# Moving the next sequence's output projection ahead of the previous tail's last norm, a reordered begin and a fifth ring slot

## Chip, cores and metric

One core of a Trainium2 chip runs the kernel. The metric is the device time of one execution in microseconds (us): the median over the runs of the kernel before is 3390.8 us, the lowest is 3381.3 and the highest 3396.3.

## The reference

The input x is four sequences of 512 tokens with 512 channels, and there is a second input ctx with 256 channels. Six blocks follow each other, each with a residual and a layer norm:

```python
x = _layernorm(x + _L0_attn_ref(x, ...))            # gated state-space scan + output projection, then an FFN (1408)
x = _layernorm(x + _L0_xattn_ref(ctx_1024, x, ...)) # scan over ctx, 512 channels, gated by silu(x)
x = _layernorm(x + _L0_ffn_ref(x, ...))             # 8 experts, top 2, and a shared expert
x = _layernorm(x + _L1_attn_ref(x, ...))            # attention inside segments of 4 tokens
x = _layernorm(x + _L1_xattn_ref(x, ctx_1024, ...)) # x mixed with softmax(query @ key.T) of ctx
x = _layernorm(x + _L1_ffn_ref(x, ...))             # top-8 router, scales x and adds a bias row
```

The scans are `h = exp(dt * A) * h + dt * B * u; y = sum_n h * C` over time, with 16 states for each channel.

## The kernel before

The kernel works through four sequences b = 0 to 3. A sequence has three parts. The **front** norms x (tasks p_sq and p_nrm), projects it (p_mm, 16 chunks of 128 channels), convolves (p_ev) and makes dt, B and C. A short front for ctx (c_load, c_mm, c_ev, c_th, c_bc) does the same for the second scan. The **scans** are three units of 512 channels (unit q = 3b is the ctx scan, 3b + 1 and 3b + 2 are the two halves of the x scan), each with 16 steps, one for each state: on the vector engine (DVE) a step is the multiply by B (L1303), the scan itself (L1386) and the multiply by C (L1394); TensorE (PE) spreads the rows of B (L675) and C (L781) over the partitions into PSUM; the scalar engine (ACT) makes the exponentials (L1007); GpSimd (POOL) adds up over states (L1664). A unit opens with dt_mm, dt_exp, dt_b and dt_c and, for the x units, ends with fin (L1398), which gates the result into `yg`.

The **tail** of a sequence is one long dependent chain: the output projection mix (L804, eight half-chunks of eight matmuls), x1 (L1413, adds x), t_sq and t_rs (mean of squares with a matmul by ones, L811, and the norm, L1419), the FFN (L830 and L837 up, L665 down), two layer norms, the gate, routing (L907), 15 expert blocks (transposes L847, gate and up L854 and L858, down L873), the shared expert (L665), the segment attention (L951, L962), xmix (L968), norm 4, the router of the last block (bias_a, L975), bias_b and bias_c (L987), bias_d (adds L1600, statistics L1604), bias_y (L1613) and the output (L592). In tail b the first matmul of mix waits for the statistics of bias_d of tail b - 1, because both use PSUM banks 0 to 4, and x1 and t_rs wait for the previous output, which is stored from T2.

All four engines run instructions strictly in an order that `plan()` and `schedule()` write at build time: `plan()` lists tasks with a rank (lower goes first), a duration and predecessors, and `schedule()` simulates a list scheduler. The semaphore waits in the code keep it right whatever the durations are. While tail b runs, the scans of sequence b + 1 and its front run too, on the same engines. Weights stream from HBM on the sync engine's (SP) queue into a ring of NSLOT slots of 512 KB; a load waits until the slot's last user is done. On the same queue stand the outputs and, once, the relay: 57 copies from DRAM to DRAM (`egu`, `xrows`) that lay out the expert weights, placed between the sixteen loads of fold. Fold (L789, L791) folds attention weights once, after the front of sequence 0. At the start SP loads `pk` (constants) and `eb`; ACT loads X, then a few small pieces, waits for the DVE set-up to finish (`set`), and only then issues the loads of hx (V) and ctx (L1028, L1034). c_mm of sequence 0 uses one PSUM bank for its four chunks and waits for each convolution; dt_mm does the same with bank 5.

Buffers that matter: V holds the residual sum x1, then hx of the next front, ctx and the attention matrix of xmix; T2 holds the normed input and then `nat`, the running value of the tail; T1 holds FFN temporaries, p_sq's squares and the scaled value of bias_b.

Of the kernel before, what the change touches and what calls it, by code (L numbers as in the profile page):

```python
# [16 lines left out]
P = 128  # L17
# [21 lines left out]
NSLOT, SLOT = 4, 1024  # L39
# [16 lines left out]
for _n, _c in _PACK:  # L56
# [9 lines left out]
       "h_done": 2, "delta": 3, "hx_in": 16, "ctx_in": 16, "tctx_in": 16, "x_in": 16, "out_done": 16 * TT,  # L66
# [15 lines left out]
def plan():  # L82
# [16 lines left out]
    for q in range(UNITS):  # L99
# [3 lines left out]
        for k in range(4):  # L103
            after = [(("dt_mm", q, k - 1), "act")] if k else [last, ready, (("sa", first - 2, 0), "act") if q else None]
            chain(15, ("dt_mm", q, k), [("pe", 0.9), ("act", 1.45)], *after)
# [65 lines left out]
    for b in range(SEQS):  # L171
        at = (("bias_d", b - 1, 0), "dve") if b else (("folded", 0, 0), "dve")
        for m in range(2 * KC):
            at = chain(30, ("mix", b, m), [("pe", 3.6)], at, (("fin", 3 * b + 2, 0), "dve"))
            if m % 2:
                chain(30, ("x1", b, m // 2), [("dve", 0.7)], at, (("bias_y", b - 1, 0), "dve") if b else None)
        if b:
            put(30, ("out", b - 1, 0), "pe", 0, (("mix", b, 2 * KC - 1), "pe"))
# [3 lines left out]
        at = chain(30, ("t_rs", b, 0), [("act", 2.7), ("dve", 2.9)], (("t_sq", b, 0), "pe"))  # L182

        def hidden(kind, chunks, at, us):

            for c in chunks:
                wait = []
                if c - 2 >= chunks[0]:
                    wait.append(((kind + "_ev", b, c - 2), "dve"))
                put(30, (kind + "_mm", b, c), "pe", 3.6, at, *wait)  # L190
# [3 lines left out]
                      (("c_bc", 1, 0), "dve") if kind == "ffn" and b == c == 0 else None)  # L194
# [52 lines left out]
        for k in range(FA):  # L247
# [14 lines left out]
        chain(60, ("att_qk", b, 0), [("pe", 5), ("act", 1.4)], (("t_load", b, 0), "act", 4),  # L262
              (("p_gz", b + 1, 2 * UC - 1), "dve") if b + 1 < SEQS else None)
        row = (("att_qk", b, 0), "act")
# [28 lines left out]
def lender(task):  # L293
# [5 lines left out]
    if t in ("p_bc", "p_bb") and n == 0:  # L299
        return t, b, 1  # L300
    if t in ("dt_mm", "c_mm") and n == 0:
# [5 lines left out]
    return task if t in ("c_bc", "fold", "att_qk", "bg", "bd") else None  # L307


def schedule():  # L310
# [44 lines left out]
    [f"slot{i}" for i in range(NSLOT)] + ["pk_in", "memz", "pm_in", "aneg", "set"] +  # L355
    ["x_in", "hx_in", "ctx_in", "tctx_in", "out_done"] +
# [14 lines left out]
def build(nc, pack, w_in, w_x, w_bc, w_dt, x_in_w, x_proj_w, x_dt_w, w_out, w_fgu, w_fdn, w_egu, w_edn,  # L371
# [3 lines left out]
    with ExitStack() as ctx:  # L375
# [61 lines left out]
        att, nat, ynat = V, T2, T2  # L437
# [1325 lines left out]
```

## Time and profile before

| what | value |
|---|---|
| median of 3 runs | 3390.8 us |
| profiled execution, time | 3388.9 us |
| profiled execution, span | 3387.1 us |
| PE busy | 2446.5 us (72%) |
| DVE busy | 2505.5 us (74%) |
| ACT busy | 1237.5 us (37%) |
| POOL busy | 1049.0 us (31%) |
| mean granted TensorE clock | 0.825 |
| mix of sequence 0 starts (L804) | 640.3 us |
| unit 5 ends (L1398) | 1319.5 us |
| unit 8 ends | 1999.0 us |
| unit 11 ends | 2717.6 us |
| scan instructions L1386 | 192, mean 4511 ns |

The spans are those of one profiled execution. A window row gives the stretch, its length, and then for each engine the busy time and in brackets the number of instructions, then the granted clock (1.00 is full, 0.50 is half), the mean busy share of the 16 DMA engines and what they moved. A chain row is one piece of the chain of work that ended last. In a timeline row the bracket at the end gives how long the engine stood idle before it and what released it.

### The profile page before, as it was taken

How to read it: one execution, taken by the hardware profiler on the slowest of the kernel's cores; microseconds unless marked ns; L12 is line 12 of the kernel's file. 1: busy time of each engine (PE TensorE's matmuls, PEld its weight loads, DVE VectorE, ACT ScalarE, POOL GpSimd, SP SyncE). 2: the span in 40 equal slices, each digit the busy share in tenths (PEclk: the TensorE clock that was granted, in tenths of full speed). 3: DMA queues.
4: the chain of work that ended last, by engine and by line, in shares of the span. 5: the costliest groups of instructions: out<-in, count | busy, mean ns of one | idle time of the engine just before them, and what ended most of it. 6: DMA issues, size and time to landing. Idle time of an engine off the chain costs nothing. (4 is left out here: it accounts for less than half of the span.)

```text
span 3387.1 us, 20370 instructions
## 1 busy us (share of the span) xinstructions
PE 2446.5 (72%) x6316; PEld 1167.2 (34%) x6316; DVE 2505.5 (74%) x1928; ACT 1237.5 (37%) x1970; POOL 1049.0 (31%) x291
## 2 busy tenths in 40 slices
PE   4775121589788864699787865699788867979875
PEld 1232000234344432334433432344434433444432
DVE  2986989899699988996988979966989922121023
ACT  3433232443534534344425454324434322021122
POOL 0233544434245353332344433412353410000000
PEclk8775555699889976799889986799799977979986
DMA  2163000111226630122126630122136611215730
GB/s 85 33 194 109 0 6 0 31 59 55 69 74 207 212 106 6 50 64 69 50 97 202 201 104 0 51 71 72 40 121 208 205 55 50 69 46 192 252 112 13
DMA packets 151196, 307.87 MB, mean 91 GB/s; under 512 B 29808, under 2 KB 47216, under 8 KB 150000
## 3 DMA queue, kind: packets, MB, share of 16 engines
q1 hardware_dynamic: 130864, 261.41, 24.8%
q10 hardware_dynamic: 15104, 28.38, 2.4%
q0 software_dynamic: 5120, 16.78, 1.5%
q8 instruction: 51, 0.84, 0.1%
q14 instruction: 57, 0.47, 0.0%
HBM read 278.21 MB, written 43.78 MB: 95 GB/s over the span
## 5 line engine op out<-in xcount | busy, mean ns | idle before, releaser
L1664 POOL TENSOR_TENSOR ya<-ya,hb 128x2048 f32<-128x2048 f32 x188 | 859.8, 4574 | 1375.7 <-DVE hb L1386 1295.7
L1386 DVE TENSOR_TENSOR_SCAN hb<-da,hb 128x2048 f32<-128x2048 f32 x192 | 866.1, 4511 | 1.3
L1007 ACT ACTIVATE da<-dl,pk 128x511 f32<-128x511 f32 x768 | 489.3, 710 | 562.2 <-DVE hb L1386 545.5
L1303 DVE TENSOR_TENSOR hb<-du,ps 128x2048 f32<-128x2048 f32 x192 | 435.7, 2269 | 28.8 <-PE ps L675 17.2
L1394 DVE TENSOR_TENSOR hb<-hb,ps 128x2048 f32<-128x2048 f32 x192 | 437.4, 2278 | 0.6
L675 PE MATMUL ps<-bct,sel 64*128 64x512 f32 x192 | 112.2, 584 | 332.1 <-DVE hb L1303 327.1
L704 PE MATMUL ps<-V,ring 128*128 128x512 f32 x512 | 246.0, 634 | 23.7 <-DVE ucv L1284 13.0
L665 PE MATMUL ps<-ring,hid 128*128 128x512 f32 x544 | 242.5, 600 | 3.2 <-ACT X L1172 1.6
L854 PE MATMUL ps<-ring,hid 128*128 128x352 f32 x480 | 199.6, 499 | 48.7 <-DMA ring<-egu 40.5
L858 PE MATMUL ps<-ring,hid 128*128 128x352 f32 x480 | 193.0, 485 | 12.3 <-ACT X L1172 11.9
L675 PEld LDWEIGHTS ps<-bct,sel 64*128 64x128 f32 x192 | 40.8, 213 | 459.4 <-DVE hb L1303 369.7
L781 PE MATMUL ps<-bct,sel 64*128 64x512 f32 x192 | 105.2, 548 | 127.3 <-DVE hb L1394 127.1
L873 PE MATMUL ps<-ring,X 128*128 128x512 f32 x360 | 177.1, 625 | 11.9 <-DMA ring<-in_w_edn 10.1
L830 PE MATMUL ps<-T,ring 128*128 128x512 f32 x352 | 167.1, 619 | 16.8 <-DVE T L1419 16.4
L837 PE MATMUL ps<-T,ring 128*128 128x512 f32 x352 | 159.1, 594 | 0.0
L704 PEld LDWEIGHTS ps<-V,ring 128*128 128x128 f32 x512 | 101.8, 204 | 157.7 <-issue 147.4
L665 PEld LDWEIGHTS ps<-ring,hid 128*128 128x128 f32 x544 | 101.9, 191 | 134.8 <-issue 129.4
L998 ACT ACT_TABLE_LOAD x44 | 56.5, 1283 | 237.8 <-DVE mv L1254 179.8
L1436 DVE SCALAR_TENSOR_TENSOR T<-T,ps 128x352 f32<-128x352 f32 x60 | 30.5, 509 | 141.7 <-ACT T L1160 141.7
L804 PE MATMUL ps<-yg,ring 128*128 128x512 f32 x256 | 121.8, 636 | 11.1 <-DVE sm L1604 10.1
L1649 POOL TENSOR_TENSOR dl<-dl,hb 128x2048 f32<-128x2048 f32 x12 | 57.3, 4779 | 231.5 <-ACT hb L1118 231.5
L1149 ACT ACTIVATE T<-ps 128x512 f32<-128x512 f32 x68 | 40.3, 596 | 240.0 <-PE ps L830 239.8
(242 smaller groups left out, 3439.6 us busy)
## 6 DMA issues: line engine op xcount, KB each, us to landing
ring<-egu SPq DMA_DIRECT2D x240, 352.0 KB, 3.4
ring<-in_w_edn SPq DMA_DIRECT2D x72, 512.0 KB, 4.9
ring<-in_w_fgu SPq DMA_DIRECT2D x44, 512.0 KB, 3.6
ring<-in_w_in SPq DMA_DIRECT2D x32, 512.0 KB, 3.6
hid<-xrows SPq DMA_DIRECT2D x60, 256.0 KB, 3.5
yrows<-X ACTq DMA_DIRECT2D x60, 256.0 KB, 4.2
ring<-in_w_egu SPq DMA_DIRECT2D x24, 512.0 KB, 3.3
ring<-in_w_edn SPq DMA_DIRECT2D x60, 192.0 KB, 4.4
```

The costliest lines, as they stand in the source:

```text
L665: i = pe.matmul(ps[:, e, :], hid[:, k - lo, e * P:(e + 1) * P], cur["down"][:, base:base + HID], start=(k == lo), stop=(k == hi - 1 and do ...
L704: i = pe.matmul(ps[:, 4 + 2 * (n % 2), :], cur["w"][:, o:o + P], hx[:, k, :], start=(k == 0), stop=(k == KC - 1))
L830: i = pe.matmul(ps[:, b0, :], w[:, k * P:(k + 1) * P], src[:, k, :], start=(k == 0), stop=(k == KC - 1))
L837: i = pe.matmul(ps[:, 2 * (n % 2) + 1, :], cur["gu"][:, o:o + P], src[:, k, :], start=(k == 0), stop=(k == KC - 1))
L854: pe.matmul(ps[:, 2 * (j % 2), 0:FE], xt(j)[:, k * P:(k + 1) * P], w[:, 0:FE], start=(k == 0), stop=(k == KC - 1))
L858: pe.matmul(ps[:, 2 * (j % 2) + 1, 0:FE], xt(j)[:, k * P:(k + 1) * P], w[:, FE:2 * FE], start=(k == 0), stop=(k == KC - 1)).then_inc(s["bg ...
L873: x = pe.matmul(ps[:, 2 * (j % 2) + 1, :], ht_(j)[0:rows, f:f + P], w[0:rows, o:o + HID], start=(i == 0), stop=(i == len(FB) - 1))
L1007: i = act.activation(dav(n % 2)[:, k, 1:], dl[:, k, 1:], ACT.Exp, scale=Aneg[:, (4 * (u % 3 - 1) if u % 3 else UC) + k, m:m + 1])
L1303: dve.tensor_tensor(hbv(m % NHB), du[:, :, :], wide(ps[:, 5, :], 4), ALU.mult).then_inc(s["dbu"], 1)
L1386: dve.tensor_tensor_scan(hb[:, h, :], da[:, b % 2, :], hb[:, h, :], 0.0, ALU.mult, ALU.add)\
L1394: dve.tensor_tensor(hbv(h), hbv(h), wide(ps[:, 7, :], 4), ALU.mult).then_inc(s["hc"], 1)
L1664: pool.tensor_tensor(sums, ya[:, :, :], hbv(m % NHB), ALU.add).then_inc(s["acc"], 1)
```

## The change

The ring gets a fifth slot. At the begin, ACT issues the loads of ctx and hx first, X follows later, and `eb` and the whole relay move behind the load of dt_mm of unit 2. In sequence 0, c_mm and dt_mm of unit 0 use four PSUM banks. The output projection of sequence b may start as soon as xmix of tail b - 1 is done (and fin, and the next ctx front): it uses banks 4 and 6 in turn, its x1 adds in place to a copy of x that a new load x_load brings into V, the squares go to `hid`, their sum to bank 4. The output is stored from T1, so waits for the stored output move from x1 and t_rs to the next front's p_sq and the FFN's first two chunks; the FFN's first matmul takes over the wait for bias_d. att_qk becomes two tasks, with the same instructions. The diff, cut to its core ("..." marks what is left out of a line):

```diff
-NSLOT, SLOT = 4, 1024
+NSLOT, SLOT = 5, 1024
@@ plan(): dt_mm, c_mm
-            after = [(("dt_mm", q, k - 1), "act")] if k else [last, ready, ...]
+            after = [(("dt_mm", q, k - 1), "act" if q else "pe")] if k else [last, ready, ...]
-            put(60, ("c_mm", b, n), "pe", 1.8, (("c_ev", b, n - 1), "dve") if n else (("c_load", b, 0), "act", 4),
+            put(60, ("c_mm", b, n), "pe", 1.8, (("c_ev", b, n - 1), "dve") if n and b else (("c_load", b, 0), "act", 4), ...
@@ plan(): output projection
-        at = (("bias_d", b - 1, 0), "dve") if b else (("folded", 0, 0), "dve")
+        at = (("xmix", b - 1, TT - 1), "pe") if b else (("folded", 0, 0), "dve")
+        put(30, ("x_load", b, 0), "act", 0.1, (("xmix", b - 1, TT - 1), "pe") if b else (("p_mm", 0, 2 * UC - 1), "pe"))
-            at = chain(30, ("mix", b, m), [("pe", 3.6)], at, (("fin", 3 * b + 2, 0), "dve"))
+            at = chain(30, ("mix", b, m), [("pe", 3.6)], at, (("fin", 3 * b + 2, 0), "dve"),
+                       (("x1", b, m // 2 - 2), "dve") if m >= 4 else None,
+                       (("c_bc", b + 1, 0), "dve") if b + 1 < SEQS else None)
-                chain(30, ("x1", b, m // 2), [("dve", 0.7)], at, (("bias_y", b - 1, 0), "dve") if b else None)
-        if b:
-            put(30, ("out", b - 1, 0), "pe", 0, (("mix", b, 2 * KC - 1), "pe"))
+                chain(30, ("x1", b, m // 2), [("dve", 0.7)], at, (("x_load", b, 0), "act", 4.5))
-        at = chain(30, ("t_rs", b, 0), [("act", 2.7), ("dve", 2.9)], (("t_sq", b, 0), "pe"))
+        at = chain(30, ("t_rs", b, 0), [("act", 2.7), ("dve", 2.9)], (("t_sq", b, 0), "pe"),
+                   (("bias_b", b - 1, 0), "act") if b else None)
+        if b:
+            put(30, ("out", b - 1, 0), "pe", 0, (("bias_y", b - 1, 0), "dve"))
@@ hidden(): the first two FFN chunks of b
+                    wait.append((("bias_d", b - 1, 0), "dve"))
@@ build(): storage, loads
-        att, nat, ynat = V, T2, T2
+        att, nat, ynat = V, T2, T1
+                    if b == 2:
+                        n += [("relay", e, 0) for e in range(EXP)]
-                    if i % 2:
-                        n.append(("relay", i // 2, 0))
-                sp.dma_start(eb[:, :], ebias).then_inc(s["pk_in"], 16)
+                            sp.dma_start(eb[:, :], ebias).then_inc(s["eb_in"], 16)
@@ tensor engine
-                        else:
+                        elif b:
                             pe.wait_ge(*of("h_conv", b, n))
-                            i = pe.matmul(ps[:, 6, :], cur["c"][:, o:o + P], cx(b)[:, k, :],
+                            i = pe.matmul(ps[:, 6 if b else n, :], cur["c"][:, o:o + P], cx(b)[:, k, :],
-                        pe.matmul(ps[:, 5, :], cur["d"][0:rows, n * P:(n + 1) * P], low[0:rows, :],
+                        pe.matmul(ps[:, 5 if q else n, :], cur["d"][0:rows, n * P:(n + 1) * P], low[0:rows, :],
@@ tensor engine, mix
-                            if b:
-                                pe.wait_ge(*of("bn", b - 1, 1))
+                            if b + 1 < SEQS:
+                                pe.wait_ge(*of("h_bc", b + 1, 2))
+                        elif half == 0 and m >= 2:
+                            pe.wait_ge(*of("x1", b, m - 1))
-                            i = pe.matmul(ps[:, m, :], cur["mix"][:, k * P:(k + 1) * P], yg[:, k, :],
+                            i = pe.matmul(ps[:, 4 + 2 * (m % 2), :], cur["mix"][:, k * P:(k + 1) * P], yg[:, k, :],
@@ t_sq
-                            i = pe.matmul(ps[:, 0, :], ones, T1[:, k, :], start=(k == 0), stop=(k == KC - 1))
+                            i = pe.matmul(ps[:, 4, :], ones, hid[:, k, :], start=(k == 0), stop=(k == KC - 1))
@@ ffn_mm, n == 0
+                                if b:
+                                    pe.wait_ge(*of("bn", b - 1, 1))
@@ scalar engine
-                act.dma_start(X[:, :, :], xT[0]).then_inc(s["x_in"], 16)
+                act.dma_start(cx(0), ctxT[0]).then_inc(s["ctx_in"], 16)
+                act.dma_start(hx[:, :, :], xT[0]).then_inc(s["hx_in"], 16)
@@ p_sq, n == 0
-                            if b:
-                                act.wait_ge(*of("stat", b - 1, 1))
+                            if b >= 2:
+                                act.wait_ge(*of("out_done", b - 2, 16 * TT))
+                    elif t == "x_load":
+                        if b:
+                            act.wait_ge(*of("down", b - 1, 16))
+                        else:
+                            act.wait_ge(*of("h_mm", b, 20))
+                        act.dma_start(V[:, :, :], xT[b]).then_inc(s["xv_in"], 16)
@@ ffn_ev, first two chunks
+                        elif b:
+                            act.wait_ge(*of("out_done", b - 1, 16 * TT))
@@ vector engine, x1 and t_rs
-                        dve.tensor_tensor(V[:, n, :], ps[:, n, :], X[:, n, :], ALU.add).then_inc(s["x1"], 1)
+                        dve.tensor_tensor(V[:, n, :], ps[:, 4 + 2 * (n % 2), :], V[:, n, :], ALU.add).then_inc(s["x1"], 1)
-                            dve.wait_ge(*of("out_done", b - 1, 16 * TT))
+                            dve.wait_ge(*of("xs", b - 1, TT))
@@ gpsimd, t_sq
+                        pool.wait_ge(*of("x_in", b, 16))
```

## Rows read from the trace of the kernel before

**Rows 1.** Windows: busy us of each engine, granted clock, DMA share, GB/s.

```profile
200.00:285.00 85.00, 67.66 (x176) 37.91 (x174) 65.54 (x40) 19.78 (x31) 32.24 (x7) 0.55 0.78 223
285.00:640.00 355.00, 79.33 (x98) 25.55 (x98) 317.35 (x111) 119.70 (x172) 163.37 (x38) 0.51 0.02 6
1330.00:1404.00 74.00, 44.62 (x111) 22.83 (x110) 69.55 (x68) 25.21 (x44) 22.73 (x6) 0.64 0.04 15
1404.00:1600.00 196.00, 184.61 (x421) 76.90 (x421) 159.58 (x112) 83.75 (x117) 63.26 (x14) 0.97 0.22 72
2120.00:2300.00 180.00, 150.12 (x331) 62.72 (x331) 135.13 (x126) 57.23 (x83) 49.87 (x10) 0.88 0.19 61
2715.00:2838.00 123.00, 70.52 (x202) 41.44 (x201) 40.35 (x90) 31.20 (x63) 9.90 (x9) 0.69 0.12 39
3081.00:3247.00 166.00, 136.97 (x447) 73.88 (x445) 16.31 (x31) 33.10 (x62) 0.00 (x0) 0.98 0.76 240
```

**Rows 2.** Chain of waits, sequences 2 to 3: start, us, what.

```profile
2783.26 16.83 PE ps L968 x32
...
2813.38 7.10 PE ps L975 x32
2827.56 7.21 PE ps L987 x8
...
2838.14 30.40 PE ps L804 x64
2868.54 3.45 PE ps L811 x8
2875.57 6.42 PE ps L830 x8
```

**Rows 3.** Timeline of the begin: start, us, engine, line, operation [idle before].

```profile
18.07 0.45 ACTq L1034 DMA_DIRECT2D hid<-in_ctxT  x1
27.68 0.78 ACT L1066 ACTIVATE yb<-ps,pk 128x512 f32<-128x512 f32 x1 [13.91 <-PE ps L743]
28.50 2.31 DVE L1284 SCALAR_TENSOR_TENSOR yb<-ps,pk,yb 128x511 f32<-128x511 f32 x3 [10.84 <-ACT yb L1066]
34.58 0.78 ACT L1066 ACTIVATE yb<-ps,pk 128x512 f32<-128x512 f32 x1 [3.11 <-PE ps L743]
...
51.58 5.25 PE L751 MATMUL ps<-yb,ring 128*64 128x512 f32 x8 [3.27 <-issue]
...
70.98 5.86 PE L704 MATMUL ps<-V,ring 128*128 128x512 f32 x8
...
96.00 4.42 DVE L1386 TENSOR_TENSOR_SCAN hb<-da,hb 128x2048 f32<-128x2048 f32 x1
```

**Rows 4.** DVE's waits, window 96 to 285: total us, times, longest.

```profile
DVE hb L1303 <- PE ps L675: 17.2, 4, 9.1
```

**Rows 5.** Page, DMA issues: count, KB each, us to landing.

```profile
ring<-in_w_in SPq DMA_DIRECT2D x32, 512.0 KB, 3.6
ring<-in_w_qo SPq DMA_DIRECT2D x16, 512.0 KB, 5.9
```

**Rows 6.** Timeline of the change from sequence 0's tail to 1's.

```profile
1344.64 3.17 PE L968 MATMUL ps<-V,X 128*128 128x512 f32 x7
...
1399.23 12.48 PE L804 MATMUL ps<-yg,ring 128*128 128x512 f32 x24 [3.38 <-DVE sm L1604]
...
1447.85 2.90 PE L830 MATMUL ps<-T,ring 128*128 128x512 f32 x3 [4.27 <-DVE T L1419]
```

**Rows 7.** The same change, sequence 1's tail to 2's.

```profile
2092.50 3.17 PE L968 MATMUL ps<-V,X 128*128 128x512 f32 x7
...
2149.53 2.90 PE L804 MATMUL ps<-yg,ring 128*128 128x512 f32 x3 [3.38 <-DVE sm L1604]
```

**Rows 8.** PE's waits, window 3081 to 3247.

```profile
PE ps L854 <- DMA ring<-egu: 23.9, 15, 2.7
```

**Rows 9.** A window of 2 us within one block of the last tail.

```profile
3126.00:3128.00 2.00, 0.84 (x3) 0.64 (x4) 0.00 (x0) 0.00 (x0) 0.00 (x0) 1.00 1.01 340
```

More of the change, by code:

```diff
@@ L103, in plan @@
         for k in range(4):
-            after = [(("dt_mm", q, k - 1), "act")] if k else [last, ready, (("sa", first - 2, 0), "act") if q else None]
+            after = [(("dt_mm", q, k - 1), "act" if q else "pe")] if k else [last, ready, (("sa", first - 2, 0), "act") if q else None]
             chain(15, ("dt_mm", q, k), [("pe", 0.9), ("act", 1.45)], *after)
@@ L300, in lender @@
         return t, b, 1
+    if t == "att_qk" and n == 0:
+        return t, b, 1
     if t in ("dt_mm", "c_mm") and n == 0:
@@ L353 @@
 SIGNALS = (
-    [f"slot{i}" for i in range(NSLOT)] + ["pk_in", "memz", "pm_in", "aneg", "set"] +
-    ["x_in", "hx_in", "ctx_in", "tctx_in", "out_done"] +
+    [f"slot{i}" for i in range(NSLOT)] + ["pk_in", "eb_in", "memz", "pm_in", "aneg", "set"] +
+    ["x_in", "xv_in", "hx_in", "ctx_in", "tctx_in", "out_done"] +
     ["h_stat", "h_mm", "h_tr", "h_tstat", "h_bstat", "h_dtm", "b_row", "c_row",
@@ L920, in _ @@
                     elif t == "att_qk":
-                        w = slot()
-                        pe.wait_ge(*of("tctx_in", b, 16))
-                        if b + 1 < SEQS:
-                            pe.wait_ge(*of("h_gz", b + 1, UC))
-                        if b + 2 < SEQS:
-                            pe.wait_ge(*of("h_bc", b + 2, 2))
-                        for g in range(2):
-                            if g:
-                                pe.wait_ge(*of("qk_sb", b, 1))
-                            for k in range(CC):
-                                o = (g * CC + k) * P
-                                i = pe.matmul(ps[:, 6, :], w[:, o:o + P], tcx[:, k, :],
-                                              start=(k == 0), stop=(k == CC - 1))
-                            i.then_inc(s["qk"], 1)
+                        if n == 0:
+                            cur["qk"] = slot()
+                            pe.wait_ge(*of("tctx_in", b, 16))
+                            if b + 1 < SEQS:
+                                pe.wait_ge(*of("h_gz", b + 1, UC))
+                            if b + 2 < SEQS:
+                                pe.wait_ge(*of("h_bc", b + 2, 2))
+                        else:
+                            pe.wait_ge(*of("qk_sb", b, 1))
+                        for k in range(CC):
+                            o = (n * CC + k) * P
+                            i = pe.matmul(ps[:, 6, :], cur["qk"][:, o:o + P], tcx[:, k, :],
+                                          start=(k == 0), stop=(k == CC - 1))
+                        i.then_inc(s["qk"], 1)
                     elif t == "att_row":
@@ L1064, in _ @@
                                 act.wait_ge(*of("g2", b - 2, TT))
-                            dst, bank, w, bias = yb(b)[:, n, :], 6, "conv_wB", "conv_bB"
+                            dst, bank, w, bias = yb(b)[:, n, :], 6 if b else n, "conv_wB", "conv_bB"
                         act.activation(dst, ps[:, bank, :], ACT.Identity, bias=c(bias, n),
@@ L1101, in _ @@
                         act.wait_ge(s["h_dtm"], 4 * q + n + 1)
-                        act.activation(dl[:, n, :], ps[:, 5, :], ACT.Relu, bias=bias)
-                        act.activation(hbv(1)[:, n, :], ps[:, 5, :], ACT.Abs, bias=bias).then_inc(s["dt_abs"], 1)
+                        bank = 5 if q else n
+                        act.activation(dl[:, n, :], ps[:, bank, :], ACT.Relu, bias=bias)
+                        act.activation(hbv(1)[:, n, :], ps[:, bank, :], ACT.Abs, bias=bias).then_inc(s["dt_abs"], 1)
                     elif t == "skip":
@@ L1199, in _ @@
                     elif t == "att_qk":
-                        for g, (dst, bias) in enumerate(((qT, "bq"), (kT, "bk"))):
-                            act.wait_ge(*of("qk", b, g + 1))
-                            act.activation(dst, ps[:, 6, :], ACT.Identity, bias=c(bias)).then_inc(s["qk_sb"], 1)
+                        dst, bias = ((qT, "bq"), (kT, "bk"))[n]
+                        act.wait_ge(*of("qk", b, n + 1))
+                        act.activation(dst, ps[:, 6, :], ACT.Identity, bias=c(bias)).then_inc(s["qk_sb"], 1)
                     elif t == "att_row":
```

58 lines of the change are left out of this document (32 added, 26 removed).

## The prediction

> **What bounds the kernel now.** I read the windows first [rows 1]. They show two regimes. Up to 2715 us DVE is the busiest engine, but not evenly: it works 94% of the stretch 1330 to 1404 (69.55 of 74 us) and only 81% of 1404 to 1600 (159.58 of 196) and 75% of 2120 to 2300 (135.13 of 180), where PE is at 94% and 83%. After 2715 there are no scans left, DVE idles, and what remains is the dependent chain of tail 2's end and of tail 3. So the kernel is bound by DVE where scans are ready, by the tail's own latency elsewhere, and the stretches in which DVE idles come right after an output projection: the scans of the ctx unit run out before the next front, which waits for the projection and its norm, has delivered.
>
> Second, the chain of waits [rows 2]. Between sequences 2 and 3 it is PE alone, one piece behind the other: xmix ends at 2783.26 + 16.83 = 2800.1, mix starts at 2838.14 and the first FFN matmul at 2875.57. The reader should see two serial pieces, 38.0 us of last norm, router and bias, and 37.4 us of mix (30.40), squares (3.45) and norm, which have no data in common. In the window 2715 to 2838 PE is busy for 57% (70.52 of 123). The same two pieces stand after the earlier tails: sequence 0 to 1, 1347.8 to 1399.2 to 1447.9, or 51.4 and 48.6 us [rows 6]; sequence 1 to 2, 2095.7 to 2149.5, or 53.8 us [rows 7]. They are longer there because scans share the engines.
>
> **The begin.** ACT issues the ctx load at 18.07, after the DVE set-up, though nothing needs to hold it; the first ACT evacuation comes at 27.68 [rows 3]. With ctx on its way from the first microsecond ACT can start it when it is free, about 17.7: 10 us earlier. Then the four chunks follow each other every 6.9 us (34.58 less 27.68), since the next matmuls wait for the convolution. With a bank for each only DVE is serial: 2.31 us of convolution and some 0.7 for the product (an estimate by the size of the 512-column operations), 3.05 per chunk, so 17.7 + 0.8 + 4 x 3.05 = 30.7 instead of 51.58 for the next matmul, 20.9 us. dt_mm of unit 0 in four banks saves a little more, but the first scan at 96.00 stands behind convolutions of the x front, which begins at 70.98 and moves with the same 21 us. I take 21. Bounds: 10 if only the load helps, 27 if dt_mm adds all it can. Up to the first mix nothing but the chain of DVE follows, so the gain passes on. The x load, moved ahead of the small loads, is twice the size of ctx; if it delays the constants, that is the lower bound.
>
> **The relay.** In 200 to 285 DVE is busy for only 65.54 of 85 us, the DMA share is 0.78 and they move 223 GB/s [rows 1]. The fold loads land in 5.9 us, where equal ones take 3.6 [rows 5]; PE waits for them, the row matmul L675 stands behind in PE's order, and DVE waits 17.2 us for it [rows 4]. Without the 57 copies between them, the folds wait little. What remains is at most one fold ahead of a row matmul, so I take 11 of the 17.2; bounds 0 and 17. The copies themselves, some 15 MB or 70 us at 223 GB/s, go to a stretch of 355 us with a DMA share of 0.02 [rows 1]. On SP they stand ahead of the load of unit 3 and of mix's weights, which are wanted only at about 600. They cost nothing there; if that cover were gone, the 70 us would stand before the first mix. `eb` is read first in the last bias step of tail 0: nothing.
>
> **The projection, sequence 3.** From 2800.1, PE has to do ln_t (3.7, an estimate by its 16 transposes), bias_a 7.10, bias_b about 1, bias_c 7.21, mix 30.40 and squares 3.45 [rows 2]: 52.9 us. After bias_c DVE still adds and takes the statistics, about 3.3, before the FFN may touch banks 0 to 3; a piece of mix, 3.8 us, may stand before a piece of the chain once or so. The FFN then starts at about 2800.1 + 52.9 + 3.3 + 2 = 2858.3 instead of 2875.57: 17 us. Bounds: 8, if the squares and the norm (7.0 from 2868.54 to 2875.57) come last, and 24, if no piece delays another and the fuller PE shortens its own matmuls.
> That last point is a clock matter: the window 2715 to 2838 shows a granted clock of 0.69, a mean of the two levels 1.2 and 2.4 GHz, with PE idle for 43%; 1404 to 1600, with PE at 94%, shows 0.97 [rows 1]. The Trainium skill, "TensorE: Matmul & The Clock Gate", section "What's actually happening", says that the default state is throttled and activity releases it. By that rule the interleaved router and bias matmuls would run at the upper level and sequence 3 would give some 4 us more; the sum doesn't use it.
>
> **Sequences 1 and 2.** Here the norm chain (51.4 and 53.8) and the projection chain (48.6) also lie side by side now. PE has room while the norm runs (44.62 of 74 busy [rows 1]). The FFN's start moves by 48.6 less some 9 us of interleaving: 39. But DVE can't give all of it: what it idles from 1330 to 1600 is 4.5 + 36.4 = 40.9 us, and a full DVE still idles 3 to 6%. 229.1 us of work at 94% take 243.7, a gain of 26; I take 27. For sequence 2 the idle time is 44.9 in 2120 to 2300 alone, 135.13 us at 94% take 143.8, a gain of 36; the chain gives at most 39, and x1 and the normed input now fall into DVE's full stretch, so I take 30. Bounds: 0 and 39 for each. Sequence 0 has no tail in front: nothing.
> New waits. PE waits for x1 of two chunks before, and behind it stand the row matmuls of the scans. x1 comes 7.6 us of matmuls earlier, and a scan on DVE takes 4.4, so this costs little. ACT's p_sq waits for the stored output of the tail before, with the exponentials behind it; the output follows bias_y, which is over by then if the order is roughly kept. SP's output wait moves ahead of some FFN loads; the fifth slot is ahead of it. POOL's wait for X is for a load issued in bias_b, long landed. x_load adds 4 MB in stretches with a DMA share of 0.04 to 0.12. All these at nothing, at most 3 us each.
>
> **The fifth slot.** In tail 3's expert blocks PE waits 23.9 us for gate and up weights, 15 times [rows 8]. The windows show the DMA engines at 0.76 and 240 GB/s in the mean [rows 1] but at 1.01 and 340 GB/s while PE waits [rows 9]: they are full in bursts and idle between, because a load can't start before a slot is free. A slot more fills the troughs, but can't make the bursts faster. I take 14, bounds 0 and 24. In the other tails DVE hides most; I take nothing.
> The Trainium skill, "DMA: Bandwidth & Descriptors", section "Specifications", gives about 358 GB/s as the HBM limit of a core; the 340 measured here agree. By that rule the mean could still rise from 240 by up to 49%, and the slot would take all 24 us; the sum keeps 14.
>
> **Sum.** 21 + 11 + 27 + 30 + 17 + 14 = 120 us off the profiled 3388.9, or 3268.9. The median before is 1.9 above the profiled run: **3271 us**, 3.5% faster. By the bounds of each, with not all at one end, this case reaches from 3235 to 3310.
>
> **Rivals.**
> - *DVE gives it back.* The projection moves, but the scans of sequences 1 and 2 lose in the norm's stretch what they win later, as DVE is 94% busy there. Against it stand the 25% idle of 2120 to 2300. It costs 57: 3328, from 3310 to 3350.
> - *The order doesn't do it.* The new list keeps the projection's pieces behind the norm's, all of rank 30. Then 74 us go: 3345. If the front's later place also eats the begin's gain, it ends at about 3375.
> - *More than the sum.* The earlier front also starts the x units earlier and closes idle time outside the windows that I counted, and each part comes near its upper bound: 3215.
> - *Slower.* p_sq's wait for the stored output stands on ACT before the exponentials, the output stands behind bias_y on a full DVE, and SP waits for it before it loads FFN weights. Each scan step that DVE misses costs 9 us (2.3 + 4.4 + 2.3). It decides from 5 missed steps at each of the three boundaries on, 45 x 3 = 135 against 120; at 6 it gives 3271 + 162 = 3433. Its ground is that ACT's order is fixed; against it, bias_y needs only bias_d's statistics and a short norm, and mix and its norm took 48.6 us from there to the FFN [rows 6].
>
> **How the numbers follow.** Chances: forecast 0.57, given back 0.18, order 0.10 (half of it near no change), more 0.08, slower 0.07. About 0.5%, 17 us, is what a measurement of this kernel can tell from no change. So faster 0.88, same 0.05, slower 0.07. The range 3225 to 3345 holds the forecast, nearly all of the first rival and part of the third.
>
> **What would show it.** Begin: the first scan near 75 us instead of 96, the first mix near 608 instead of 640. Relay: no 17 us wait for L675, and a DMA share above 0.15 in 285 to 450. Projection: matmuls L804 right after xmix, between those of L975 and L987, and the FFN of sequence 3 58 us after xmix instead of 75. DVE above 88% after the second and third mix. The slot: PE's wait for gate and up weights near 10 us in the last tail. I am wrong if the periods from mix to mix, 750 us now, shrink by less than 15, if p_sq or x1 shows a wait of tens of us, or if the tail of sequence 3 keeps its length.

## The result, and the profile after

| | before | after |
|---|---|---|
| median of all runs on the same chip | 3388.5 us | 3244.2 us (3241.5 to 3250.0) |
| ratio, with its 95% interval | | 0.9576 (0.9550 to 0.9603) |
| profiled execution | 3388.9 us, span 3387.1 | 3242.2 us, span 3240.4 |

The change takes 144 us off, 4.2%; 120 were forecast, and the time lies in the range. Where it came from shows in the milestones of each sequence, read from the timelines (us from the start of the span; "xmix" is the end of the tail's last matmul group, "mix" and "FFN" are the first matmuls of the output projection and of the FFN that follow):

| | first scan | mix 0 | FFN 0 | xmix 0 | FFN 1 | xmix 1 | FFN 2 | xmix 2 | FFN 3 | end |
|---|---|---|---|---|---|---|---|---|---|---|
| before | 96.0 | 640.3 | 689.9 | 1347.8 | 1447.8 | 2095.7 | 2198.2 | 2800.1 | 2875.6 | 3387.1 |
| after | 62.3 | 602.9 | 652.5 | 1300.0 | 1362.4 | 2015.9 | 2078.4 | 2701.1 | 2750.9 | 3240.4 |

Differences of neighbours give the sum: 37.4 up to the first mix and 10.4 in tail 0. The three stretches from xmix to FFN shrink by 37.6, 40.0 and 25.7. Tails 1 and 2 then give back 5.6 and 20.8 (647.9 to 653.5, 601.9 to 622.7), and tail 3 is 22.0 shorter. Together 146.7, the difference of the two spans.

The windows of after, over the stretches that answer to [rows 1] (start:end, length, busy us and number of instructions of PE, weight loads, DVE, ACT, POOL, granted clock, DMA share, GB/s):

```profile
200.00:285.00 85.00, 59.28 (x163) 33.45 (x162) 62.22 (x39) 30.64 (x41) 32.43 (x8) 0.63 0.57 177
285.00:450.00 165.00, 33.17 (x40) 11.01 (x40) 151.03 (x52) 54.94 (x80) 77.23 (x18) 0.50 0.22 59
1362.00:1560.00 198.00, 190.08 (x455) 81.42 (x455) 174.70 (x123) 87.89 (x126) 63.51 (x15) 0.98 0.25 82
2078.00:2260.00 182.00, 173.25 (x391) 71.93 (x391) 148.09 (x106) 76.51 (x106) 50.08 (x12) 0.98 0.26 82
2684.00:2751.00 67.00, 57.86 (x165) 27.77 (x165) 25.83 (x62) 18.52 (x32) 4.50 (x1) 0.91 0.19 63
2953.00:3092.00 139.00, 130.24 (x443) 72.48 (x442) 16.32 (x31) 32.56 (x61) 0.00 (x0) 1.00 0.90 287
```

The relay's copies now run from 255.8 to 317.7, behind the fold's loads. PE is nearly full after each boundary (96 and 95%), and DVE, at 81 and 75% before, is at 88% (174.70 of 198) and still only 81% (148.09 of 182) in the same places. The next to last row is the end of tail 2 with the projection of sequence 3 in it: PE busy for 86% at a clock of 0.91. (Between xmix and the end of the projection alone, 2701 to 2738, the granted clock is 1.00; from xmix to mix before, 2800 to 2838, it was 0.53.) In the last row the DMA engines move 287 GB/s through tail 3's blocks, 240 before.

The chain of waits at that boundary (start, us, what; mix is now L815, xmix L980, the norm's transposes L905, the router L987, the last bias steps L993 and L1000, the FFN L842), against [rows 2]:

```profile
2684.11 16.99 PE ps L980 x32
2701.09 10.30 PE ps L815 x24
2711.39 1.75 PE ps L905 x16
2713.14 3.44 PE ps L815 x8
2716.58 3.52 PE ps L987 x32
2720.10 6.92 PE ps L815 x16
2727.02 0.44 PE ps L993 x4
2727.46 3.44 PE ps L815 x8
2730.89 3.64 PE ps L1000 x8
...
2735.28 2.48 DVE sm L1629 x4
...
2743.67 1.46 DVE T L1638 x3
...
2745.63 5.21 DMA ring<-in_w_fgu
...
2750.88 5.73 PE ps L842 x8
```

The projection's pieces (L815) lie between those of the norm and the router, as the list of the change says. The group L987 takes 3.52 and L1000 3.64, where the same groups took 7.10 and 7.21 when they stood alone. And a link is there that the forecast did not have: before the FFN PE waits for its weights, not for the norm (8.25 us of idle time, ended by the load).

### The profile page after: what moved, and what is told of

Read it like the earlier page. It is cut to its first block, busy times and chain, and to the rows that moved or that the text cites. A ratio compares the mean times of both kernels' runs of the same rounds, so it can differ in the third digit from the quotient of the medians.

```text
span 3240.4 us, 20396 instructions
## 1 busy us (share of the span) xinstructions
PE 2410.5 (74%) x6316; PEld 1156.1 (36%) x6316; DVE 2482.0 (77%) x1928; ACT 1236.3 (38%) x1970; POOL 1044.1 (32%) x291
## 4 chain that ended last, share of the span: by engine, by line
PE 35%; DVE 31%; issue 18%; ACT 9%; DMA 4%; POOL 3%; ACTq 0%; SPq 0%; DVEq 0%; POOLq 0%
DVE hb L1413 12%; PE ps L842 6%; PE ps L849 6%; DVE hb L1421 4%; DVE hb L1330 4%; PE ps L713 3%; PE ps L674 3%; DMA ring<-in_w_edn 2%; PE ps L885 2%; PE ps L980 2%; POOL ya L1690 2%; PE ps L776 2%; DVE sm L1274 1%; PE ps L815 1%; DVE hb L1396 1%
## 5 line engine op out<-in xcount | busy, mean ns | idle before, releaser
L1330 DVE TENSOR_TENSOR hb<-du,ps 128x2048 f32<-128x2048 f32 x192 | 435.9, 2270 | 33.1 <-POOL ya L1690 25.2
L713 PE MATMUL ps<-V,ring 128*128 128x512 f32 x512 | 242.7, 627 | 25.7 <-DVE yg L1371 11.0
L842 PE MATMUL ps<-T,ring 128*128 128x512 f32 x352 | 166.9, 619 | 23.9 <-DVE T L1444 15.6
L713 PEld LDWEIGHTS ps<-V,ring 128*128 128x128 f32 x512 | 100.4, 201 | 155.6 <-issue 134.8
L674 PEld LDWEIGHTS ps<-ring,hid 128*128 128x128 f32 x544 | 102.4, 191 | 138.5 <-issue 132.6
L870 PEld LDWEIGHTS ps<-ring,hid 128*128 128x128 f32 x480 | 94.8, 203 | 83.4 <-ACT X L1199 33.8
L815 PE MATMUL ps<-yg,ring 128*128 128x512 f32 x256 | 116.1, 607 | 0.9 <-DVE yg L1425 0.9
```

Of the source, the lines that this page charges most:

```text
L674: i = pe.matmul(ps[:, e, :], hid[:, k - lo, e * P:(e + 1) * P], cur["down"][:, base:base + HID], start=(k == lo), stop=(k == hi - 1 and do ...
L713: i = pe.matmul(ps[:, 4 + 2 * (n % 2), :], cur["w"][:, o:o + P], hx[:, k, :], start=(k == 0), stop=(k == KC - 1))
L842: i = pe.matmul(ps[:, b0, :], w[:, k * P:(k + 1) * P], src[:, k, :], start=(k == 0), stop=(k == KC - 1))
L870: pe.matmul(ps[:, 2 * (j % 2) + 1, 0:FE], xt(j)[:, k * P:(k + 1) * P], w[:, FE:2 * FE], start=(k == 0), stop=(k == KC - 1)).then_inc(s["bg ...
L1330: dve.tensor_tensor(hbv(m % NHB), du[:, :, :], wide(ps[:, 5, :], 4), ALU.mult).then_inc(s["dbu"], 1)
```

## The experiments

All are the kernel after with one part undone, unless another base is named. "After" is the profiled execution above. Differences of spans and milestones compare one execution with one other, and some of them are scatter: in seven kernels whose begin is that of after, or differs from it only by the number of slots, the first mix lies anywhere from 602.1 to 610.3 us and the first scan from 62.0 to 65.7. The ratios are each to runs of the kernel before on the same chip; that of after is 0.9576 (0.9550 to 0.9603).

### The projection back behind the norm, in all boundaries, in two, in one

```diff
-        at = (("xmix", b - 1, TT - 1), "pe") if b else (("folded", 0, 0), "dve")
+        at = (("bias_d", b - 1, 0), "dve") if b == 3 else (("xmix", b - 1, TT - 1), "pe") if b else (("folded", 0, 0), "dve")
```

This is the kernel for sequence 3 alone; the others have `b` (all) and `0 < b < 3` in place of `b == 3`.

> The changed kernel, only its plan is altered: the projection of sequences 1, 2 and 3 is listed behind bias_d of the tail in front, as before; storage, waits, ring and begin stay changed. My theory (the gain lies in the order): in the changed kernel the stretch from xmix's end to the next FFN shrank by 37.6, 40.0 and 25.7 us and tails 1 and 2 gave 5.6 and 20.8 back, so this kernel loses 77: about 3321 us, with the first projection unmoved at about 603 us. Rival 1 (the separate storage does it and the order hardly matters): 3244 to 3255. Rival 2 (what was given back came from something else, the order is worth the full 103): 3347.

Measured: 3331.6 us, ratio to before 0.981 (0.978 to 0.984), span 90.4 above after. Of these, 7.4 stand before the first mix (610.3), where this edit changes nothing; behind it 83.0 are left.

> The changed kernel with the projections of sequences 1 and 2 alone listed late. Theory (the two give 77.6 us at their place, and DVE takes 26 of them back in tails 1 and 2, where it then has more scans left): 3244 + 51 = 3295. Rival 1 (they pass on in full): 3322. Rival 2 (where scans run DVE is the bound and nothing passes on): 3244 to 3255.

Measured: 3303.0 us, 0.972 (0.969 to 0.975), span 64.8 above. xmix to FFN is 34.3 and 41.7 longer (FFN at 1396.7 and 2161.0), 76 in all; at xmix 2 64.7 are left, at 2765.8 instead of 2701.1. The tails take back only 11, not the 26 expected: tail 2 takes 604.8, 18 less than in after, but tail 1 takes 660.1, nearly 7 more.

> The changed kernel with the projection of sequence 3 alone listed late. No scans are left here, so what it gave at its place passes on: 25.7 us, about 3270. Of these I take 18 for matmuls in idle time and 7 for the clock: then the last router and bias matmuls of tail 2, L987 and L1000, are back at about 7 us each from 3.7. Rival (the clock had another cause): those stay at 3.7 and the kernel is at 3262.

Measured: 3265.5 us, 0.962 (0.959 to 0.964), span 24.0 above. xmix 2 ends at 2701.3, as in after, and the FFN starts 73.2 us behind it instead of 49.8. Its chain of waits, same columns as above:

```profile
2684.31 17.00 PE ps L980 x32
...
2714.62 7.10 PE ps L987 x32
...
2728.80 7.19 PE ps L1000 x8
2735.99 30.46 PE ps L815 x64
...
2774.52 5.37 PE ps L842 x8
```

The two long durations are back, and the granted clock from xmix to mix (2701 to 2736) is 0.54, as it was before. The parts give 64.8 + 24.0 = 88.8, all three together 90.4, or 83.0 from the first mix on. So the order by itself is worth 83 to 90 us of the 147 in these profiles. The ratios, 0.981 against 0.958, say 79.

### Do idle matmuls give the clock's share without the projection?

On the kernel before, matmuls whose result nobody reads, ahead of the norm's last group, of bias_a and of bias_b, in the tails of sequences 2 and 3 (the last of the three places is shown; the others have 12 and 4 matmuls):

```diff
+                        if b >= 2:
+                            for _ in range(10):
+                                pe.matmul(ps[:, 6, :], ones, fill512, start=True, stop=True)
```

> The kernel before, with matmuls that compute nothing of use put into PE's idle time in the last norm and router of tails 2 and 3 (12, 4 and 10 of 128x512, into a bank that nobody reads), the result unchanged. Theory of the clock (idle PE is why L975 and L987 took 7.1 and 7.2 us, and interleaved work is why they take 3.7 in the changed kernel): in tail 2 they go to 3.7 each, in tail 3 to 3.7 from 5.4 and 7.2, in all 12 us: 3388 less 12 = 3376. Rival (the clock has another cause, or the added matmuls delay the chain as much as they give): 3388 or more.

Measured: 3388.3 us, 0.998 (0.997 to 1.000). Its chain of waits (here the fillers are L893, L978 and L988, router and bias L982 and L997, mix L805):

```profile
2799.40 10.30 PE ps L893 x24
...
2811.45 3.44 PE ps L978 x8
2814.88 3.52 PE ps L982 x32
2818.40 8.64 PE ps L988 x20
...
2828.25 3.71 PE ps L997 x8
...
2835.33 29.78 PE ps L805 x64
```

The durations fall as expected, 7.10 to 3.52 and 7.21 to 3.71, and the granted clock of the stretch is 0.96 instead of 0.53. But from xmix's end to mix it takes 35.9 us instead of 38.0, and to the FFN 72.7 instead of 75.5: of some 7 us that the groups save only 2.8 arrive. PE runs its instructions in order, so 10.30 + 3.44 + 8.64 us of fillers stand in the chain themselves, where only part of that was idle before. The profiled span is 11.7 us shorter all the same, but this execution lies 11 us under the median of ten, and 5.0 of it come from the last tail's blocks (146.8 us from the first to the last matmul of the down projections, instead of 151.8), where no filler runs. The ratio says 0.2%, by its interval 0.0 to 0.3%. So the 12 us expected did not come, and the rival, that the added matmuls cost about what they give, was nearer: I had counted them as filling waits alone. In the change the fillers are work that has to be done anyway; that the same effect is worth its full size there is argued from this, no run separates it.

### The give-back: is tail 2 longer because DVE is full?

In the C multiply of all three units of sequence 3 only a quarter of the channels is multiplied (this leaves out a part of the scan's output), so each of these 48 multiplies takes 0.68 us instead of 2.28, and DVE has less to do beside tail 2:

```diff
-                        dve.tensor_tensor(hbv(h), hbv(h), wide(ps[:, 7, :], 4), ALU.mult).then_inc(s["hc"], 1)
+                        m4 = 1 if b >= 9 * NST else 4
+                        dve.tensor_tensor(hbv(h)[:, 0:m4], hbv(h)[:, 0:m4], wide(ps[:, 7, :], m4), ALU.mult).then_inc(s["hc"], 1)
```

> The changed kernel in which the 48 scan steps of sequence 3 multiply only a quarter of the channels by C (a part of its scan output is not computed): 48 x 1.7 = 80 us less for DVE, nearly all inside tail 2. Theory (tail 2 became 20.8 us longer, 622.7 from FFN start to xmix end, since 48 us more of DVE work fall into it): tail 2 shrinks by 30 us or more, to under 595, kernel about 3244 less 35 = 3209. Rival (PE or the loads made tail 2 longer, DVE is not its bound): tail 2 stays within 8 us of 622.7.

Measured: 3213.0 us, 0.947 (0.944 to 0.949). FFN 2 starts at 2074.9 and xmix 2 ends at 2676.5: 601.6 us, against 622.7 in after and 601.9 in before. The window 2078 to 2626, first of this kernel, then of after:

```profile
2078.00:2626.00 548.00, 464.08 (x1259) 222.29 (x1257) 448.14 (x341) 233.29 (x376) 214.81 (x60) 0.92 0.39 124
```

```profile
2078.00:2626.00 548.00, 472.31 (x1246) 224.75 (x1246) 484.86 (x326) 222.48 (x351) 211.89 (x60) 0.92 0.39 124
```

With 36.7 us less on DVE in this window, tail 2 gives back nothing. The 21.1 us are short of the 30 expected, and far outside the rival's 8. More of the scans fall into tail 2 of after: 39 scan steps start in it, 34 in before, and DVE works 509.6 us in it, against 461.8 in before and 463.9 in this kernel. The length goes with DVE's work; PE is at 85 and 86% in the two windows. For tail 1 this is not shown: it gave back 5.6, but with the projections late (x_late_b12 above) DVE had 8 us less to do in it and it took 6.7 us longer still. That part stays open.

### The fifth slot

On after, `NSLOT` 5 to 4:

> The changed kernel with four ring slots, for the loads and for the plan. Theory: the fifth slot is worth what tail 3's expert blocks lost, 27 us from 166 to 139, and some of the 10 us by which tail 0 is shorter: 3244 + 27 to 37 = 3271 to 3281, and PE waits about 24 us for gate and up weights in the blocks of tail 3. Rival (DMA was at its limit and the shorter blocks come from the clock or chance): 3244 to 3255.

Measured: 3265.6 us, 0.963 (0.960 to 0.966), span 21.7 above, and the last tail's blocks (first to last down matmul, as above) take 147.6 us instead of 125.2. On before, the slot alone, with the plan still made for four (`NSLOT` 5, and `len(lent) >= 4`, `lent[-4]` in the function that makes it):

> The kernel before with a fifth ring slot in storage and loads, its plan unchanged (it still plans with four). Theory: the slot alone takes 22 to 27 us off tail 3's expert blocks and little elsewhere: 3388 less 22 = 3366, PE's wait for gate and up weights in the blocks of tail 3 falls from 23.9 to about 2. Rival (it needs the new order): 3380 to 3388.

Measured: 3364.6 us, 0.992 (0.989 to 0.995), span 27.7 below before, and the last tail's blocks take 127.5 us instead of 151.8. PE's waits over those blocks (line waited at, for what: total us, times, longest), in this order: after, after with four slots, before with five:

```profile
PE ps L885 <- DMA ring<-in_w_edn: 6.2, 10, 1.4
PE ps L866 <- DMA ring<-egu: 1.6, 3, 0.8
```

```profile
PE ps L866 <- DMA ring<-egu: 23.1, 16, 2.5
PE ps L885 <- DMA ring<-in_w_edn: 3.8, 4, 1.6
```

```profile
PE ps L873 <- DMA ring<-in_w_edn: 4.9, 8, 1.3
PE ps L854 <- DMA ring<-egu: 3.1, 6, 1.0
```

From either side the slot is worth 22 to 24 us in the blocks, all of [rows 8], and 22 to 28 in the whole span. With four slots xmix 0 also ends 7.6 us later than in after, most of the 10.4 that tail 0 gained; but before with five slots has the same tail 0 as before (657.7 us), so the slot does this only together with the rest of the change. xmix 2 is only 0.7 later (2701.8): tails 1 and 2 have made it up by then, through what is not shown.

### The three parts of the begin

Relay copies back between the fold loads:

```diff
-                    if b == 2:
-                        n += [("relay", e, 0) for e in range(EXP)]
...
+                    if i % 2:
+                        n.append(("relay", i // 2, 0))
```

> The changed kernel with the relay's copies between the fold loads again. Theory: DVE waits some 17 us for L684 again in the fold, the first projection comes 11 us later than 602.9, and the kernel is at 3244 + 11 = 3255, less what DVE slack absorbs. Rival (with five slots the folds are fed anyway): first projection within 3 us of 602.9, 3244.

Measured: 3250.5 us, 0.958 (0.956 to 0.961); first mix at 609.3, 6.4 later than after. That is within the scatter named above. Counted from the first scan on, which takes part of the scatter out, this kernel takes 547.3 us to the first mix, the ten others with the copies moved 539.4 to 544.9. The loads of fold land in 6.1 us here, in 3.4 in after, as in 5.9 before [rows 5]. DVE's wait for the row matmul, by relay back, then in after (window 60 to 285):

```profile
DVE hb L1330 <- PE ps L684: 8.3, 3, 4.2
```

```profile
DVE hb L1330 <- PE ps L684: 5.5, 3, 2.9
```

It was 17.2 in before [rows 4]. The larger part of that wait is gone even with the copies in the old place. Either edit alone does that. Before with five slots, copies and begin as they were, has the first row for 96 to 285; after with four slots, copies moved, has the second for 60 to 285:

```profile
DVE hb L1303 <- PE ps L675: 9.6, 4, 4.3
DVE hb L1330 <- PE ps L684: 4.5, 3, 2.9
```

The ctx and x loads back behind the set-up, X first:

```diff
-                act.dma_start(cx(0), ctxT[0]).then_inc(s["ctx_in"], 16)
-                act.dma_start(hx[:, :, :], xT[0]).then_inc(s["hx_in"], 16)
+                act.dma_start(X[:, :, :], xT[0]).then_inc(s["x_in"], 16)
```

> The changed kernel with the loads of ctx and hx issued behind the DVE set-up again and X first, banks as changed. Theory: the first evacuation of ctx comes at about 28 us instead of 19.6, everything up to the first projection moves by these 8 to 10 us: first projection at about 612, kernel 3253. Rival (the load order is hidden by the set-up): first projection 603, 3244.

Measured: 3250.4 us, 0.958 (0.955 to 0.960); first mix at 611.2, 8.3 later. The first evacuation comes 8.0 us later than in after (27.61 for 19.61). The first evacuation and the first scan of this kernel (start, us, engine, line, operation, idle before):

```profile
27.61 0.78 ACT L1083 ACTIVATE yb<-ps,pk 128x512 f32<-128x512 f32 x1 [13.78 <-PE ps L752]
...
70.73 4.42 DVE L1414 TENSOR_TENSOR_SCAN hb<-da,hb 128x2048 f32<-128x2048 f32 x1
```

One PSUM bank again for the four chunks of the ctx front and for unit 0's dt matmuls:

```diff
-                            i = pe.matmul(ps[:, 6 if b else n, :], cur["c"][:, o:o + P], cx(b)[:, k, :],
+                            i = pe.matmul(ps[:, 6, :], cur["c"][:, o:o + P], cx(b)[:, k, :],
...
-                        pe.matmul(ps[:, 5 if q else n, :], cur["d"][0:rows, n * P:(n + 1) * P], low[0:rows, :],
+                        pe.matmul(ps[:, 5, :], cur["d"][0:rows, n * P:(n + 1) * P], low[0:rows, :],
```

with the waits and predecessors that belong to one bank.

> The changed kernel with one PSUM bank for c_mm of sequence 0 and dt_mm of unit 0 again, loads as changed. Theory: the four chunks take 6.9 us each again instead of 3: the next matmul is 12 us later and the first scan, with dt_mm in one bank, 16 to 20 us later than 62.3; first projection at about 617, kernel 3258. Rival (DVE is the bound up to there, so an earlier first scan is only an earlier first scan): first projection within 4 us of 602.9.

Measured: 3264.6 us, 0.962 (0.959 to 0.964), span 22.7 above; first mix at 627.4, 24.5 later, where 617 was expected. The timeline of the begin, first with one bank, then in after:

```profile
19.65 0.78 ACT L1082 ACTIVATE yb<-ps,pk 128x512 f32<-128x512 f32 x1 [4.30 <-DVE T L1351]
26.33 0.78 ACT L1082 ACTIVATE yb<-ps,pk 128x512 f32<-128x512 f32 x1 [2.89 <-PE ps L752]
...
43.10 5.21 PE L760 MATMUL ps<-yb,ring 128*64 128x512 f32 x8 [3.27 <-issue]
...
62.46 5.84 PE L713 MATMUL ps<-V,ring 128*128 128x512 f32 x8
...
62.56 0.69 ACT L1119 ACTIVATE dl<-ps,pk 128x512 f32<-128x512 f32 x1 [2.16 <-PE ps L776]
...
87.47 4.43 DVE L1413 TENSOR_TENSOR_SCAN hb<-da,hb 128x2048 f32<-128x2048 f32 x1
```

```profile
19.61 1.45 ACT L1082 ACTIVATE yb<-ps,pk 128x512 f32<-128x512 f32 x2 [4.30 <-DVE T L1351]
...
30.90 5.44 PE L760 MATMUL ps<-yb,ring 128*64 128x512 f32 x8 [11.98 <-DVE yb L1311]
...
38.65 4.44 PE L776 MATMUL ps<-bcf,ring 16*128 16x512 f32 x8 [2.30 <-DVE bct L1392]
...
62.30 4.42 DVE L1413 TENSOR_TENSOR_SCAN hb<-da,hb 128x2048 f32<-128x2048 f32 x1
...
67.51 9.40 PE L713 MATMUL ps<-V,ring 128*128 128x512 f32 x16 [4.04 <-DVE V L1358]
```

Up to the matmul L760 the banks give 12.2 us (43.10 to 30.90). To the first scan they give 25.2, although the x front (L713) starts 5 us later in after. With one bank unit 0's dt chunks (L776, evacuated at L1119) go from PE to ACT one by one, and are still at it at 62.56, when the x front has begun. With four PE does all eight matmuls in one go at 38.65, and the first scan stands ahead of the front and its convolutions. (The run undoes both bank edits at once; that the 13 us behind L760 come from the dt matmuls is read from the timelines.) The three parts give 6.4 + 8.3 + 24.5 = 39.2 at the first mix, where after has 37.4. Against a scatter of up to 8 us only the banks' 24.5 are large; in the whole time the kernels with relay or loads back, at ratios of 0.958 each, can't be told from after.

With the order's 83 to 90, the slot's 22 and these 37.4 little is left of the 146.7. No run takes back the split of att_qk or the separate storage of the projection.

### SP's wait for the stored output

The new link in the chain: SP stores the finished output of sequence 2 before it asks for the FFN weights of sequence 3, and waits for bias_y to do so. DVE starts to apply the norm at 2745.34, the load is issued at 2745.63 and PE starts at 2750.88. Here the store goes behind the loads of the next FFN's first two chunks:

```diff
-                    n.append(b)
+                    held.append(b)
+                if held and (held[0] == SEQS - 1 or (t == "ffn_mm" and b == held[0] + 1 and i >= 1) or past(held[0], t, b, i)):
+                    n.append(held.pop(0))
```

> The changed kernel with the output stores of the tail in front behind the loads of the next FFN's first two chunks on SP's queue. In the changed kernel PE waits 8.2 us for the first FFN weights of sequence 3, which SP issues only at 2745.6, after it waited for bias_y. Theory: the FFN starts right after its norm, at about 2746.4 instead of 2750.9, 4.5 us, kernel 3240. Rival (the output then comes late for the waits on it and p_sq or the FFN evacuation pays): no gain or 5 to 10 us more.

Measured: 3239.3 us, 0.954 (0.952 to 0.957). xmix 2 to FFN 3 takes 45.2 instead of 49.8 us, as expected, and PE's wait now ends with the normed input (DVE T), no longer with the load:

```profile
2751.14 1.80 SPq L659 DMA_DIRECT2D ring<-in_w_fgu  x3
2751.75 4.60 PE L850 MATMUL ps<-T,ring 128*128 128x512 f32 x5 [3.61 <-DVE T L1452]
```

In the span 0.9 us arrives, and the interval overlaps that of after, so a gain in the whole time is not shown. Tail 2 ended at 2706.6 instead of 2701.1; 2.4 of these 5.5 us were there at FFN 2 already, for the rest I have no cause. The same with idle matmuls in the last tail's gaps (98 in all, 52 of them in its norm):

> The same, and matmuls that compute nothing of use in PE's idle time of tail 3 (between 3 and 20 of 128x512 before each step of its norms, gate, segment attention and router, into a bank that nobody reads), the result unchanged. Theory: L919, L963, L980, L987 and L1000 of tail 3 lose what they take over their times in full clock, about 2 + 3 + 2 + 1.7 + 3.5 = 12 us: 3228. Rival (the added matmuls run over the idle time): 3240 or more.

Measured: 3234.0 us, 0.953 (0.951 to 0.956), the lowest median of the kernels that compute everything. Its profile shows bias_a at 3.5 and bias_c at 4.6 us instead of 5.6 and 7.2, and the end 47.9 us after xmix 3 instead of 50.2; but from FFN 3 to xmix 3 it takes 440.6 instead of 437.5, and the span (3239.4) is that of the kernel without them. This execution lies 7 us above its median. The intervals overlap, so that the fillers help is not shown.

## Why the prediction was right, and where its terms were off

**The projection, the largest term (74 forecast), was right in mechanism and size.** At the places the two chains side by side gave 37.6 and 40.0, where the working had 39 each as the chain's own gain; after the give-back of tails 1 and 2 (5.6 and 20.8) and with sequence 3's 25.7, 76.9 remain. Undoing it cost 83 to 90 in the profiles, 79 by the ratios. The limit by DVE was there as well, but not where I had it. I took it off in the stretch right after the boundary, from its idle time at 94% busy. It came as a longer tail 2 instead, and DVE stood at 88.2 and 81% behind the boundaries, so "above 88%" was just reached behind the first and missed behind the second. That the sum of the term came out is in part luck: sequences 1 and 2 gave 51.2 (77.6 less 26.4) for 57, and sequence 3 made up for it with 8.7 more than its own. Of the rival "DVE gives it back" 26 of its 57 us happened; for the 20.8 of tail 2 the lighter DVE run shows the cause, for the 5.6 of tail 1 it stays open.

**Sequence 3 (17, measured 25.7; 23.4 by undoing it).** It came out just above the upper bound of 24, and by one of the reasons given there, the clock: L987 and L1000 ran in 3.5 and 3.6 instead of 7.1 and 7.2, 7 us, and the norm's transposes, bias_b and the projection itself (27.8 for 30.4) gave some 5 more. From xmix to the projection's end the granted clock is 1.00, the upper of the two levels, 2.4 GHz, where 0.53, near the lower, stood before. The lower bound's condition came true as well, without its price: the squares and the norm did come last (2738.9 to about 2746), behind the last x1. By the Trainium skill's rule ("TensorE: Matmul & The Clock Gate", "What's actually happening") I had given some 4 more than the sum: the trace agrees in sign, with a larger number. Against it ran SP's output wait, 4.6 us, which I had priced at 3 at most. Without it 30 us were there (45.2 for 75.5, in the kernel with the store moved), outside my bounds.

**The begin (21, measured 8.3 + 24.5).** The load order gave nearly what was taken (10). The banks were mis-sized: I took 11 of them. The step to L760 was right (30.7 forecast, 30.90 measured), but the next one failed, that the first scan stands behind the convolutions of the x front and moves with it, by the same 21 us. The first scan moved by 33.7, to 62.3, while the x front moved by 3.5 (70.98 to 67.51). I had looked at what the bank frees in the ctx front and not at what the same edit does to the order of unit 0's dt steps against the x front; I had bounded it at 27 in all, and it is 33 at the first mix.

**The relay (11, measured 6.4, give or take the scatter).** Two edits shared one wait, and I had given it all to one: the fifth slot alone takes the 17.2 us to 9.6, the slot with the new begin to 8.3, and moving the copies as well to 5.5. With the copies moved and four slots it is 4.5, so the mechanism (copies hold up the fold loads) was right, and what was missed is that the slot covers the same wait. The DMA share of 0.22 in 285 to 450 is as forecast.

**The fifth slot (14, measured 22 to 24).** The term was mis-sized by my choice between bounds. The sum took the middle because loads at 340 GB/s can't go faster; but it is the troughs that counted, and the mean rose from 240 to 287 GB/s, still well below 340. PE's wait for these weights fell from 23.9 to 1.6, that for the down weights rose from 3.5 to 6.2. The reading by the limit in the Trainium skill ("DMA: Bandwidth & Descriptors", "Specifications"), that the mean has room and the slot would take all 24, was the right one, and I should have gone by it. Outside tail 3 I took nothing: tail 0 gained up to 7.6 by it, of which 0.7 was left at the end of tail 2.

**The new waits.** The slower rival's mechanism is there in small. At the first and the second boundary ACT waits before it squares the input of the next front (p_sq), with the exponentials behind it (at 1377.2 and 2093.3):

```profile
1373.21 1.15 ACT L1067 ACTIVATE T<-V 128x512 f32<-128x512 f32 x2 [11.75 <-DMA out<-T]
...
2089.30 1.15 ACT L1067 ACTIVATE T<-V 128x512 f32<-128x512 f32 x2 [11.83 <-DMA out<-T]
```

It is a wait of 11.8 us each time. Most of it is not the output's: the load of that input itself (V), issued only at 1364.3 and 2080.3, lands at 1370.6 and 2086.5, the last piece of the output at 1373.1 and 2089.2. So the output adds 2.6 and 2.7 us, within the 3 priced. The slower case needed five missed scan steps, 45 us, at each boundary; 11.8 us are little more than one step's 9. POOL's add of x, "long landed" by the working, does wait for its load: POOL idles 13.2 us at the first boundary and 14.2 at the second until it lands. DVE shows no wait for POOL in either stretch, so that error cost nothing. PE's waits for x1 do not show.

**The sum.** Against 120 stand 146.7 of the span: +5.4 up to the first mix (37.4 for 32), +10.4 in tail 0 (nothing forecast), +2.9 for the projection, +8.0 in tail 3 (22.0 for 14). Half of it, 13.4, is a choice between bounds, and the 10.4 of tail 0 are a term put at nothing. For the banks and the slot I took the middle, though the rows (a DMA share of 0.76 in the mean, four chunks handed over one by one) spoke for the upper end.

## What to carry to other kernels

Two chains that share an engine but no data, each leaving it idle in turn, give most of the shorter one when they are woven together (here 37.6 and 40.0 us of some 49, and 25.7 of 37); the engine that bounds the rest can take part of it back, but in the tail behind, so it has to be looked for in the length of the next stage and not at the seam. When an in-order queue (SP's stores before loads, ACT's squares before exponentials) is moved along with the work, follow each of its waits: one of them became the last to end here. Two edits that shorten the same wait must not both be credited with it. And a separate bank or slot changes not only how long a step takes but which work comes first; cost it by who is let past.

## What the runs showed of the hardware

- Matmuls that fill an idle TensorE bring the clock up for their neighbours: the same groups took 7.10 and 7.21 us alone and 3.5 to 3.7 with other matmuls between them, at a granted clock of 1.00 and 0.96 (with the projection, with idle matmuls) instead of 0.53 between xmix and mix. But fillers that are not needed otherwise cost most of it: 2.8 us arrived of 7 in the chain, with 22 us of them in it.
- A ring of five slots of 512 KB instead of four took the DMA rate in the last tail's blocks from 240 to 287 GB/s in the mean, with single windows at 340 in before [rows 9]. The limit had been the wait for a free slot, not the bandwidth.
- Loads of 512 KB that stand between copies from DRAM to DRAM on the same queue landed in 5.9 us (6.1 with the copies back in the changed kernel), in 3.4 and 3.2 us with the copies moved behind them (five and four slots).
